# Moving the low halves of the context from VectorE to GpSimd in an attention stage, with two changes of order

## The reference

```
x  = x + attn(layernorm(x), ctx)       # attn: both quantised to fp8 in blocks of 128, then
                                       # einsum('emk,enk->emn', xq, wq) for each of 4 batches
x  = x + ffn(layernorm(x))             # 32 experts, 6 of them for each token, and a shared expert
# quantisation of x: per row and 128 columns;  of ctx: per 128 rows and 128 columns
#   q = fp8(v * 448 / max|v|);  back: q * max|v| / 448
```

## Time and profile before

| | |
|---|---|
| time, median of 3 runs | 6591.76 us (6581.7 to 6593.26) |
| the profiled execution's own time | 6590.12 us |
| its span in the profile | 6588.2 us |
| PE busy | 6347.2 us (96%) |
| DVE busy | 2004.7 us (30%) |
| ACT busy | 1330.1 us (20%) |
| POOL busy | 2900.1 us (44%) |
| granted TensorE clock, mean | 0.992 |

### The profile page before, as it was taken

One profiled execution on the slowest core, in us unless ns is written; L12 is line 12 of the kernel. 1 busy time (PEld: TensorE's weight loads), 2 busy tenths in 40 slices (PEclk: granted clock), 3 DMA queues, 4 the chain that ended last, 5 costly groups with the idle time before them and its releaser, 6 DMA issues.

```text
span 6588.2 us, 89812 instructions
## 1 busy us (share of the span) xinstructions
PE 6347.2 (96%) x32166; PEld 3137.9 (48%) x32167; DVE 2004.7 (30%) x2640; ACT 1330.1 (20%) x1976; POOL 2900.1 (44%) x2388
## 2 busy tenths in 40 slices
PE   2999999999999999999999999999999999999998
PEld 1555544445554444444444444444444444444443
DVE  7888533211112222232222222232222332223220
ACT  2666622110001111111111111111111111111111
POOL 4444523732002444454445444454444545445453
PEclk9999999999999999999999999999999999999999
DMA  2455544544335555666666565676655666667653
GB/s 87 154 156 155 178 129 88 122 108 132 109 98 152 158 159 159 164 177 176 168 171 166 164 159 158 166 196 178 170 161 158 184 192 170 168 164 187 180 151 94
DMA packets 1122342, 1015.67 MB, mean 154 GB/s; under 512 B 875504, under 2 KB 877808, under 8 KB 1122288
## 3 DMA queue, kind: packets, MB, share of 16 engines
q1 hardware_dynamic: 177920, 437.40, 20.3%
q10 hardware_dynamic: 838720, 241.77, 19.5%
q0 software_dynamic: 105648, 335.82, 16.5%
HBM read 623.21 MB, written 210.14 MB: 126 GB/s over the span
## 4 chain that ended last, share of the span: by engine, by line
PE 73%; POOL 6%; issue 5%; DVE 5%; DMA 4%; ACTq 3%; ACT 3%; POOLq 0%; DVEq 0%; SPq 0%
PE ps_gu L766 48%; PE ps_d L766 23%; DMA out<-s_out,y_now 3%; PE ps_d L969 2%; ACTq L1228 2%; POOL s_out L701 1%; POOL list_rows L652 1%; POOL hid L711 1%; ACTq L1246 1%; POOL hid_hl L716 1%; ACT wts L1117 1%; DVE wts L1452 1%; DMA xT<-xin 1%; POOL s_out L694 1%; ACT dout L1262 1%
## 5 line engine op out<-in xcount | busy, mean ns | idle before, releaser
L766 PE MATMUL ps_gu<-wts,xT 128*128 128x512 f16 (+1 forms) x20304 | 3950.6, 356 | 24.4 <-DMA xT<-xin 8.2
L766 PEld LDWEIGHTS ps_gu<-wts,xT 128*128 128x128 f16 x20304 | 1993.4, 98 | 1947.1 <-issue 27.4
L766 PE MATMUL ps_d<-wts,hT 128*128 128x512 f16 x7968 | 1768.1, 380 | 23.4 <-ACT dout L1262 11.9
L1594 DVE TENSOR_SCALAR wts<-stage 128x1408 f16<-128x1408 f32 (+2 forms) x447 | 427.6, 957 | 3180.8 <-PE ps_d L969 2995.4
L766 PEld LDWEIGHTS ps_d<-wts,hT 128*128 128x128 f16 x7968 | 778.8, 98 | 956.8 <-issue 38.7
L701 POOL TENSOR_TENSOR s_out<-s_out,dout 128x1024 f32<-128x1024 f32 x208 | 529.7, 2547 | 1218.9 <-ACT dout L1262 1215.8
L1596 DVE SCALAR_TENSOR_TENSOR wts<-stage,wts 128x1408 f16<-128x1408 f32 (+2 forms) x447 | 735.7, 1646 | 15.4
L1232 ACT ACTIVATE sil<-ps_gu 128x704 f32<-128x704 f32 (+2 forms) x272 | 199.1, 732 | 2023.8 <-PE ps_gu L766 2023.6
L1262 ACT ACTIVATE dout<-ps_d,lists 128x1024 f32<-128x1024 f32 x208 | 231.8, 1114 | 1349.7 <-issue 1338.3
L1238 ACT ACTIVATE hid_hl<-hid 128x704 f16<-128x704 f32 (+2 forms) x272 | 207.9, 764 | 1284.8 <-POOL hid L711 1224.0
L711 POOL TENSOR_TENSOR hid<-hid,sil 128x704 f32<-128x704 f32 x208 | 348.5, 1675 | 131.7 <-ACT hid L1266 127.4
(11 more groups left out here) (167 smaller groups left out, 2650.4 us busy)
## 6 DMA issues: line engine op xcount, KB each, us to landing
stage<-in_L_ffn_w_down SPq DMA_DIRECT2D x384, 256.0 KB, 4.4
stage<-in_L_ffn_w_gate SPq DMA_DIRECT2D x256, 352.0 KB, 4.0
stage<-in_L_ffn_w_up SPq DMA_DIRECT2D x256, 352.0 KB, 5.6
wts<-in_x SPq DMA_DIRECT2D x64, 512.0 KB, 3.7
rows_x<-wts SPq DMA_DIRECT2D x64, 512.0 KB, 3.2
xT<-cols_x ACTq DMA_DIRECT2D x63, 512.0 KB
wts<-in_ctx SPq DMA_DIRECT2D x32, 512.0 KB, 4.0
cols_x<-xT SPq DMA_DIRECT2D x32, 512.0 KB, 4.7
```

The source lines that it names most:

```text
L766: ins = nc.tensor.matmul(dst[c], left, right[c], start=(first and a == 0), stop=(last and a == 2))
L1594: v.tensor_scalar(high, raw, WSCALE, 1.0, ALU.mult, ALU.mult).then_inc(cast_done, 1)
```

## The change

- `ctx_low` leaves VectorE and becomes one instruction on GpSimd, last in its step. GpSimd can't read PSUM, so ScalarE's `take_ctx` now evicts the scaled tile as float32 into `ctx_f` (a piece of `hT` that is free in this stage) and then casts it from there into the high half; GpSimd subtracts the high half from `ctx_f`. A new semaphore `ctx_taken` tells TensorE that the PSUM tile is free; `ctr_free` (low half written) now also tells ScalarE that `ctx_f` is free.
- GpSimd's step begins with a wait for the rounding of the context tile, ahead of `dequantise_x`, and with `low_of_x2(i - 1)`, which was `low_of_x2(i)` at the end of the step.
- TensorE does `tr_q(i + 1)` and `tr_ctx(i + BT)` before `turn_max(i + CLEAD)`.
- In the prologue `ctx_low(c - 1)` stands on GpSimd between `unround_ctx(c)` and `split_slice(c)`.

```diff
+        ctx_f = hT_flat[:, 0:2 * H].bitcast(F32).rearrange("p (k n) -> p k n", k=KH)
@@ gpsimd
+            def ctx_low(c, j, b):
+                pool.wait_ge(ctx_high, c + 1)
+                pool.sem_inc(pool_turn, 1)
+                g.tensor_tensor(cT[b % 2][:, 1, :, ds(j * P, P)], ctx_f, cT[b % 2][:, 0, :, ds(j * P, P)],
+                                ALU.subtract).then_inc(ctr_free, 1)
-            def beside(i, ctx=True, x2=True):
+            def beside(i, ctx=True, x2=True, low=None):
+                if ctx:
+                    pool.wait_ge(rounded[CTX], i + CLEAD)
+                if x2:
+                    low_of_x2(i - 1)
                 dequantise_x(i + (LEAD - 1))
                 if ctx:
                     unround_ctx(i + (CLEAD - 1))
-                if x2:
-                    low_of_x2(i)
+                if low is not None:
+                    ctx_low(i + BT, *low)
             for c in range(BT):
                 unround_ctx(c)
+                if c > 0:
+                    ctx_low(c - 1, c - 1, 0)
                 split_slice(c)
             dequantise_x(0)
+            ctx_low(BT - 1, BT - 1, 0)
...
             for i in range(TT - CLEAD + 1, TT):
                 if i < TT - LEAD + 1:
-                    beside(i, ctx=False)
+                    beside(i, ctx=False, low=(i - 2 * BT, 3) if i < 3 * BT else None)
                 else:
+                    low_of_x2(i - 1)
+                if i == TT - 1:
                     low_of_x2(i)
@@ tensor
             def tr_ctx(c):
                 pe.wait_ge(deq_ready[CTX], c + 2)
-                pe.wait_ge(ctr_free, c + 1)
+                pe.wait_ge(ctx_taken, c + 1)
...
-                if ctx_max:
-                    turn_max(i + CLEAD)
                 tr_q(i + 1)
                 if ctx:
                     tr_ctx(i + BT)
+                if ctx_max:
+                    turn_max(i + CLEAD)
@@ scalar
                 act.wait_ge(ctr_done, c + 2)
+                act.wait_ge(ctr_free, c + 1)
                 act.sem_inc(act_turn, 1)
                 for k in range(KH):
-                    last = a.activation(cT[b % 2][:, 0, k, ds(j * P, P)], ps_t_ctx[:, k, :], ACT.Copy, scale=scale_of_ctx(c, k))
-                last.then_inc(ctx_high, 1)
+                    last = a.activation(ctx_f[:, k, :], ps_t_ctx[:, k, :], ACT.Copy, scale=scale_of_ctx(c, k))
+                last.then_inc(ctx_taken, 1)
+                act.wait_ge(ctx_taken, c + 2)
+                act.sem_inc(act_turn, 1)
+                a.activation(cT[b % 2][:, 0, :, ds(j * P, P)], ctx_f, ACT.Copy).then_inc(ctx_high, 1)
@@ vector
-            def ctx_low(c, j, b):
-                dve.wait_ge(ctx_high, c + 1)
-                dve.sem_inc(dve_turn, 1)
-                for k in range(KH):
-                    last = v.scalar_tensor_tensor(out=cT[b % 2][:, 1, k, ds(j * P, P)], in0=ps_t_ctx[:, k, :],
-                                                  scalar=scale_of_ctx(c, k), in1=cT[b % 2][:, 0, k, ds(j * P, P)],
-                                                  op0=ALU.mult, op1=ALU.subtract)
-                last.then_inc(ctr_free, 1)
...
-                if low is not None:
-                    ctx_low(i + BT, *low)
```

More of the change, by code:

```diff
@@ L269, in build @@
             for n in ("qin_in", "qin_free", "rounded", "deq_ready"))
-        unrounded_x, ctx_high = sem("unrounded_x"), sem("ctx_high")
+        unrounded_x, ctx_taken, ctx_high = sem("unrounded_x"), sem("ctx_taken"), sem("ctx_high")
         q_high = sem("q_high")
@@ L621, in _ @@
             beside(-1, x2=False)
-            beside(0)
-            beside(1)
-            with pool.Fori(2, TT - CLEAD + 1) as i:
-                beside(i)
+            beside(0, x2=False, low=(0, 1))
+            beside(1, low=(1, 1))
+            with pool.Fori(2, BT) as i:
+                beside(i, low=(i, 1))
+                add_slice(i - 2)
+            with pool.Fori(BT, 2 * BT) as i:
+                beside(i, low=(i - BT, 2))
+                add_slice(i - 2)
+            with pool.Fori(2 * BT, TT - CLEAD + 1) as i:
+                beside(i, low=(i - 2 * BT, 3))
                 add_slice(i - 2)
@@ L1074, in _ @@
             act.sem_inc(tr_free, 1)
+            act.sem_inc(ctx_taken, 1)
             act.sem_inc(norm_l, 1)
@@ L1508, in between, with beside @@
                 yield
-            def beside(i, x=True, ctx=True, low=None, sliced=True):
+            def beside(i, x=True, ctx=True, sliced=True):
                 if ctx:
@@ L1539, in _ @@
                 quantise(c=c)
-                ctx_low(c - 1, c - 1, 0)
             x_moments(0)
@@ L1543, in _ @@
             quantise(0)
-            ctx_low(BT - 1, BT - 1, 0)
             for i in (1, 2):
@@ L1552, in _ @@
                     low_of_q(0)
-            beside(0, sliced=False, low=(0, 1))
-            beside(1, sliced=False, low=(1, 1))
-            with dve.Fori(2, BT) as i:
-                beside(i, low=(i, 1))
-            with dve.Fori(BT, 2 * BT) as i:
-                beside(i, low=(i - BT, 2))
-            with dve.Fori(2 * BT, TT - CLEAD) as i:
-                beside(i, low=(i - 2 * BT, 3))
+            beside(0, sliced=False)
+            beside(1, sliced=False)
+            with dve.Fori(2, TT - CLEAD) as i:
+                beside(i)
             with dve.Fori(TT - CLEAD, 3 * BT) as i:
-                beside(i, ctx=False, low=(i - 2 * BT, 3))
+                beside(i, ctx=False)
             with dve.Fori(TT - BT, TT - LEAD) as i:
```

## The result

The kernel after takes 6610.17 us (median of 7 runs, 6602.41 to 6625.15), beside 6590.02 for the kernel before (7 runs). The ratio is 1.0038, 95% interval 1.0025 to 1.005: slower by about 20 us. The forecast was 6587, no change, with a range to 6604: both are wrong. The profiled execution took 6604.3 with a span of 6602.7.

A forecast was written before the change was run, and what follows sets the result against it. VectorE was taken to bound the attention loop, at 23.9 us a step. Prologue +7, first steps -4, periods -20.9, leaving them -1.3, boundaries +7, step 24 +2, splits +7 sum to -3.2: 6587 us, range 6562 to 6604.

The forecast's parts named there:

- Part 1: Attention loop: taking the low halves off VectorE frees nothing in steps 2 to 21, since ScalarE is late there; 0.
- Part 2: Attention loop: POOL waits for both roundings; period 23.9 to 22.8, set by the context tile's landing; -20.9, steps 0 and 1 -4.
- Part 3: Attention loop: ScalarE's float32 eviction and extra cast, 1.05 to 1.55 a step, covered by TensorE's earlier transposes; 0.
- Part 4: TensorE's transposes ahead of the turn: no gain while VectorE is the bound, except once at steps 21 to 22; -1.3.
- Part 5: Low halves on POOL: no cost in inner steps, attention waits at batch boundaries; +7 for two, +2 at steps 23 to 24.
- Part 6: Prologue: POOL and VectorE exclude each other, so a context tile takes 11.4 instead of 10.35; +6, passage to attention +1.
- Part 7: Split steps 25 to 28: low half of x2 in series on POOL, about 1.8 in each of four periods; +7.
- Rival C: Attention loop: POOL's low half reaches past R+11.8 and collides with VectorE's scale instructions; +21, 6608 us; chance 0.10.

The follow-up runs named there:

- 12: Kernel before with only the context low halves moved to GpSimd, with ScalarE's float32 tile and second cast: median 6612.0 us, ratio 1.0030.
- 8: Kernel of experiment 1 with the context tile's load ahead of the x tile's on SyncE's queue: median 6570.9 us.
- 9: Kernel of experiment 1 without POOL's wait for the context rounding at the head of its step: median 6576.6 us.
- 6: Kernel before with POOL's new order to step 23 and TensorE's transposes ahead of the turn, low halves staying on VectorE: median 6572.5 us.
- 7: Kernel of experiment 1 with TensorE's old order, turning the maximum ahead of the transposes: median 6590.8 us.
- experiment 3: Kernel after with the weight loads ahead of the store of x2 on SyncE's queue in steps 24 to 28: one execution, 6598.6 us.
- experiment 1: Kernel after with POOL's old order from step 24 on, low half of x2 ahead of the splits: median 6571.9 us, ratio 0.9981.
- Experiment 2: Kernel of experiment 1 with SyncE's store of x2 also waiting for the step's two splits in the split steps: median 6594.6 us, ratio 1.0011.

## Why the prediction was wrong, by its own steps

Part 1 (low halves off VectorE worth 0): right. VectorE waits 3.0 for ScalarE at L1514 in their place, and 12 shows the move alone as a loss.

Part 2 (periods): right. The inner period is 22.8, as forecast, and R(2) to R(21) came out within half a microsecond. The landing as the bound was right too, and 8 shows it: without it the period is 21.98, where the prediction had 21.95. But the reason "POOL waits for both roundings" was wrong for the inner steps: 9 shows that the wait is idle there, and works only in steps 0 and 1.

Part 3 (cast hidden): right, by the cover named (6, 7); its price without cover was put about twice too high.

Part 4: right, -1.4 against -1.3, and 6 shows nothing in the periods.

Part 5 (boundaries): right in size, and only in part by its mechanism. Attention step 8 began at R+10.3 (forecast R+10.8), behind a wait of 4.14 for POOL's L605, and the next R came 26.1 behind the last, within my 24.8 to 26.5. The two boundaries cost 4.4 and 4.2 over periods of 22.8, where the sum had 4.0 each (8 less the 1 that the kernel before loses). But I had laid this on POOL's later low half, with the clock as an extra. Attention began only 0.35 and 0.04 later than in the kernel before (R+9.95); the products behind the wait took 5.63 and 5.74 for 4.06, and 6 has the same loss with the low half on VectorE. R(23) to R(24) lost 4.1, not 2: 1.5 by the later start and 2.6 by the products:

```profile
307.15 5.63 PE L788 MATMUL ps_d<-wts,xin 128*128 128x512 f16 x18 [4.14 <-POOL wts L605]
...
677.11 6.67 PE L788 MATMUL ps_d<-wts,xin 128*128 128x512 f16 x18 [4.29 <-POOL wts L605]
```

Part 6 (prologue): mis-sized, by 5.7 too much, which hid a part of the miss of part 7. A tile took 10.52, not 11.4, and the start of attention moved by 1.3, not 7. The two engines do exclude each other: L1446, 8 columns, takes 1.32 and ends at 57.83 with POOL's L605 (57.79); POOL's L561 takes 2.06 (1.21 in the earlier trace rows) beside L1456, and L1461 1.58 beside L561. The sum was wrong in treating all of both engines' work as one line. POOL's first two split instructions, 1.3 together, cost VectorE's L1451 and L1456 only 0.3 and 0.4. The exclusive lock of the Trainium skill's page "SBUF — State Buffer" (section "SBUF: two separate sides") agrees with the ends of L1446 and L605; taken as "all times add" it gave the 11.4, which the trace refutes.

Part 7 (low half of x2 behind the splits): **this is the step that failed**, by 32 us. I forecast 1.8 in each of four periods: 7. The four cycles grew by 6.1 each (29.6 against 23.5), 24.5 in all, the steps on either side by 5.6, and the stretch from the last transposes of x (858.41; 841.74 before) to the mark by 9.0.

The 1.8 of the series was right for a cycle: experiment 3 has 25.5, experiment 1 23.7. Three things were left out. One is the queue. "Their readers are 10 and more away, so 0" looked at the readers of what SyncE stores, and at the loop. In the splits the queue also holds weight loads and the x tile, and all of them leave together once L610 is done, right ahead of the transposing transfer, which then lands in 5.7 instead of 2.4: 4.0 a cycle and 17.2 in all by experiment 2. TensorE then waits 4.7 to 5.4 us a cycle and its clock falls: the granted clock from 720 to 840 us is 0.90, where it was 0.97, in these windows (stretch, PE busy, instructions, clock, share of the DMA engines, GB/s) before and then after:

```profile
720.00:840.00 120.00, 111.30 (x687) 0.97 0.57 171
```

```profile
720.00:840.00 120.00, 92.88 (x545) 0.90 0.47 141
```

Experiment 2 has 0.90 too, experiment 3 0.97: the clock goes with the wait for the transfer.

The second is ScalarE. Its normalising of the next x2 tile (L1155) writes over the tile that L610 reads and waits for it: 1.8 to 2.2 us in each of the four cycles, and over 5 us in each of the last two steps with splits. No kernel with the old order has this wait.

```profile
870.66 1.24 ACT L1155 ACTIVATE dout<-wts,shift_l,scale_l 128x1024 f32<-128x1024 f32 x1 [5.15 <-POOL wts L610]
...
872.75 1.96 ACTq L1181 DMA_TRANSPOSE hT<-stage  x1
```

The third is the end, where this wait counts. In ScalarE's order the high half of the hidden slice and its transposing transfer stand behind L1155; the transfer leaves at R+13.9 instead of R+10.1, 0.5 behind the last of four transfers of SyncE's queue, and lands 7.8 behind its issue. TensorE, which had also waited 1.73 for L610, waits 3.78 for it. R(30) to R(31) takes 27.5 instead of 20.1. I had counted four periods only. Experiment 3 has the same wait (5.15) and the same period (27.6), and by it the end costs 9.5 of the series' 20.7; how much of that is the late issue and how much the slow landing was not tried.

Rival C, the slower case, named POOL's low half past R+11.8; it ended at R+10.4 and that rival didn't happen. The slowdown came by a mechanism that no rival held.

The prediction should have taken the cycle of the earlier trace rows as a chain of its own, with each of its links (POOL, SyncE's queue, ScalarE's normalising and its transfer, TensorE, ScalarE, POOL), and asked of each what the later low half moves, as it did for the loop.

## To carry to other kernels

When an instruction is moved behind others, follow everything that waits for it, to read its result or to write over its input, and the DMA queue above all: a store that waits holds the loads behind it, and they come out in a bunch in front of whatever is urgent on another queue. A kernel with several regimes needs the cost worked out in each; here the order behind the 14 us gained in the inner steps lost 39 in the steps with splits, and choosing it by step kept both. And once the bound is a tile's landing, look first at what stands ahead of its load: exchanging two loads gave 15 us by the marks, as much as the new order had given in the loop.

## What was not expected of the hardware

- A transposing transfer on ScalarE's queue takes 2.4 us to land with four transfers issued on SyncE's queue ahead of it (kernel before) and 5.7 to 6.6 with eight in 4.5 us. The number alone does not decide: behind four that had left 0.5 to 2.2 us ahead it took 7.8 (872.75, kernel after), behind four that had left 3.8 to 5.5 ahead 2.5 (experiment 3). While it was under way the DMA engines were busy 96% and 97% in two slow cases (733.60 in the kernel after, 760.38 in experiment 2) and 39% in the kernel before (767.25). That this load is what delays it fits, and was not tried apart; nor was which of the eight counts. The Trainium skill's page "DMA: Bandwidth & Descriptors" (section "Queues, rings and completion order") has both queues on the same DMA engines, taking turns by packets, which fits the sign; no run here shows the turns.
- What a wait costs in the products behind the transposing transfer is not fixed by its length. In steps 24 to 31 of all fourteen kernels the 8 products took 1.90 after every wait below 1.9 us, and 3.29 to 3.60 after every wait of 3.8 to 5.8. In between, at 1.9 to 2.9 us, they took anything from 1.90 to 3.58: after 2.90 it was 3.20 in kernel 1 and 1.90 in kernel 6. Of these, the 3.59 at 739.35 had a granted clock of 0.50. At steps 8, 16 and 24, behind waits of 3.9 to 4.3, 18 products took 5.36 to 6.99 for 4.05. So 4 us of waiting cost up to 2.9 more, over the 1.7 that I had as the most.
- VectorE's reduction over 1024 columns (L1410) took 1.21 in the prologue beside POOL's L600 (53.09 to 54.30, beside 53.38 to 55.72), as when alone, while its two-input L1456 and even L1446, 8 columns and one input, waited POOL's out. So not every pair excludes, and the number of inputs alone does not tell which.
